# Attention with the product with v a quarter slot later over three buffers, and the shift loaded ahead of the stores

## The reference

```python
q = relu(queries @ Wq_w.T + Wq_b)      # 8 batches x 512 x 128, 16 heads of 8
k = relu(keys @ Wk_w.T + Wk_b)         # one batch, 512 keys
v = relu(values @ Wv_w.T + Wv_b)
score = einsum('bhsd,bhtd->bhst', qh, kh) / sqrt(8)
attn = softmax(score, axis=-1)
a = einsum('bhst,bhtd->bhsd', attn, vh)
```

## Time and profile before

| | |
|---|---|
| median of three runs | 622.29 us (621.78 to 622.56) |
| the profiled execution | 623.81 us, of it a span of 621.3 us in the profile |
| busy over the span | PE 82%, DVE 85%, ACT 64%, POOL 31% |
| products with v (L1492) in the 32 slots | 74.6 to 405.4 us of the span |

### The profile page before, as it was taken

How to read it: one execution, slowest core, us unless ns; L and a number is a source line. 1 busy time by engine, 2 the same in 40 slices (tenths; PEclk the granted TensorE clock), 3 DMA queues, 4 the chain that set the end, 5 groups by cost and what they waited for, 6 DMA issues and landing times.

```text
span 621.3 us, 9777 instructions
## 1 busy us (share of the span) xinstructions
PE 510.5 (82%) x3468; PEld 196.5 (32%) x3475; DVE 526.5 (85%) x879; ACT 395.3 (64%) x773; POOL 194.5 (31%) x309
## 2 busy tenths in 40 slices
PE   1794799999989999999999999877768798888520
PEld 1480122222222222222222222246547664433200
DVE  4769889999999999999999996157998769899976
ACT  1643378898989888888888988525446421144252
POOL 7000212039604544043461318329456330000000
PEclk9997589999999999999999999999988899999965
DMA  9943011111221112121112200010000000000012
GB/s 232 293 141 120 24 27 30 28 38 25 69 61 46 30 32 57 49 59 37 29 36 66 64 23 9 6 50 34 1 2 1 1 1 1 1 0 28 7 34 68
DMA packets 31392, 28.93 MB, mean 47 GB/s; under 512 B 6240, under 2 KB 23784, under 8 KB 31344
## 3 DMA queue, kind: packets, MB, share of 16 engines
q1 hardware_dynamic: 29312, 27.33, 15.1%
q10 hardware_dynamic: 2032, 0.98, 0.6%
HBM read 19.23 MB, written 8.65 MB: 45 GB/s over the span
## 4 chain that ended last, share of the span: by engine, by line
PE 45%; DVE 32%; POOL 7%; ACT 7%; issue 5%; DMA 2%; ACTq 1%; SPq 0%; DVEq 0%
PE ps L1492 14%; PE ps L1487 11%; DVE row_max L1665 10%; PE ps L1460 5%; DVE space L926 4%; PE ps L585 2%; DVE space L862 2%; ACT attended L1613 2%; ACT space L1597 2%; DMA w_in<-in_L_ffn_out_proj_w 1%; DVE st L233 1%; ACT space L830 1%; POOL space L402 1%; POOL space L404 1%; PE ps L342 1%
## 5 line engine op out<-in xcount | busy, mean ns | idle before, releaser
L1665 DVE TENSOR_REDUCE row_max<-ps 128x2 f32<-128x1024 f32 x256 | 299.5, 1220 | 17.0 <-PE ps L1460 14.2
L1597 ACT ACTIVATE space<-ps 128x512 f32<-128x512 f32 x512 | 271.8, 604 | 48.3 <-PE ps L1487 47.9
L1487 PE MATMUL ps<-space 51*128 51x512 bf16 x512 | 159.2, 388 | 7.0 <-ACT space L1597 3.3
L1492 PE MATMUL ps<-space 128*32 128x512 f32 x1024 | 138.1, 612 | 2.9 <-ACT space L1597 0.7
L1460 PE MATMUL ps<-space 48*128 48x512 bf16 x512 | 128.3, 400 | 14.2 <-DVE row_max L1665 12.5
L1487 PEld LDWEIGHTS ps<-space 51*128 51x128 bf16 x512 | 41.1, 94 | 165.1 <-ACT space L1597 144.6
L1333 POOL CAST max_parts<-row_max 128x16 bf16<-128x16 f32 x32 | 6.3, 198 | 236.8 <-DVE row_max L1665 236.8
L585 PE MATMUL ps<-W,space 128*128 128x512 f32 x128 | 66.7, 603 | 0.4
L926 DVE TENSOR_REDUCE space<-ps 128x128 f32<-128x1024 f32 x32 | 38.7, 1221 | 9.1 <-PE ps L585 8.8
L448 POOL TENSOR_TENSOR space<-PC,same_row 128x512 f32<-128x512 f32 x32 | 33.0, 1064 | 35.5 <-DVE PC L876 27.4
L1460 PEld LDWEIGHTS ps<-space 48*128 48x128 bf16 x512 | 26.4, 94 | 56.1 <-DVE row_max L1665 50.2
(11 more groups left out here) (216 smaller groups left out, 623.0 us busy)
## 6 DMA issues: line engine op xcount, KB each, us to landing
q_parts_dram<-space SPq DMA_DIRECT2D x2, 1536.0 KB, 5.4
space<-q_parts_dram SPq DMA_DIRECT2D x64, 48.0 KB
attended_dram<-attended SPq DMA_DIRECT2D x128, 18.0 KB
X<-in_L_attn_queries SPq DMA_DIRECT2D x8, 256.0 KB, 7.7
space<-in_L_ffn_w SPq DMA_DIRECT2D x2, 1024.0 KB, 5.9
space<-q_parts_dram SPq DMA_DIRECT2D x64, 32.0 KB
space<-attended_dram SPq DMA_DIRECT2D x16, 128.0 KB, 2.4
space<-inverses_dram SPq DMA_DIRECT2D x16, 128.0 KB
```

The source lines that it names most:

```text
L1487: pe.matmul(ps[:, col_bank(v), :], k_rows[rows_a, kappa // 4 % 2, tc * P:(tc + 1) * P], q_stack[rows_a, kappa % 4, b * S:(b + 1) * S], sta ...
L1492: mm = pe.matmul(ps[32 * m:32 * m + 32, PV, :], v_heads[:, tc, PAIR * (kappa // 4) + m % PAIR, :], probs[:, tc % 2, m, :], start=(tc == 0) ...
L1597: act.activation(probs[:, tc % 2, m, :], ps[:, col_bank(v), :], ACT.Exp, scale=1.0 / math.sqrt(DH)).then_inc(s_pr, 1)
L1665: dve.tensor_reduce(row_max[:, par].rearrange("p (a c) -> p a c", a=PAIR)[:, :, item], ring(n), AX.X, MAX).then_inc(s_free, 1)
```

## The change

Six things are changed:

1. A third buffer of exponentials in `space8`; quarter `n = 4 kappa + tc` uses buffer `n % 3`.
2. `step` takes at its end the product with v of the quarter before instead of its own; the last product stands behind the loop. Its two waits have moved with it, into `multiply_v`.
3. ScalarE copies bank 7 of slot `kappa - 1` between the exponentials m = 2 and m = 3 of quarter 1 of slot `kappa`, instead of behind the exponentials of quarter 0. The exponential m = 3 and the turned copy now stand behind it.
4. SyncE waits for the turned copy and loads the shift ahead of the wait and the 4 stores of the slot before.
5. The turn of slot 0's maxima is at item 2 of the second eight row scores instead of item 4, with its waits.
6. ScalarE's `copy_attended` for the last slot stands behind the loop.

```diff
-        probs = view(space4, 0, [2, QB, S])
+        probs = [view(space4, 0, [QB, S]), view(space4, QB * S, [QB, S]), view(space8, 0, [QB, S])]
...
+                if kappa + 1 < NQ:
+                    sp.wait_ge(s_pr, turn_item(kappa + 1) + 1)
+                    load_shift(kappa + 1)
+
                 if kappa:
                     sp.wait_ge(s_pve, kappa)
                     store_attended(kappa - 1)
-
-                if kappa + 1 < NQ:
-                    sp.wait_ge(s_pr, turn_item(kappa + 1) + 1)
-                    load_shift(kappa + 1)
...
-            def multiply_v(kappa, tc):
+            def multiply_v(n):
+
+                kappa, tc = n // TC, n % TC
+                if tc == 0 and kappa:
+                    pe.wait_ge(s_pve, kappa)
+                pe.wait_ge(s_pr, column_item(kappa, tc, QB - 1) + 1)
                 for m in range(QB):
                     mm = pe.matmul(ps[32 * m:32 * m + 32, PV, :], v_heads[:, tc, PAIR * (kappa // 4) + m % PAIR, :],
-                                   probs[:, tc % 2, m, :], start=(tc == 0), stop=(tc == TC - 1))
+                                   probs[n % 3][:, m, :], start=(tc == 0), stop=(tc == TC - 1))
                 if tc == TC - 1:
                     mm.then_inc(s_pv, 1)
...
-                if item == 4:
+                if item == 2:
                     pe.wait_ge(s_Wc, 2)
                     pe.wait_ge(s_csum, 1)
                     turn_max(0)
...
-                if tc == 0 and kappa:
-                    pe.wait_ge(s_pve, kappa)
-                pe.wait_ge(s_pr, column_item(kappa, tc, QB - 1) + 1)
-                multiply_v(kappa, tc)
+                if kappa or tc:
+                    multiply_v(TC * kappa + tc - 1)
 
             for kappa in range(NQ):
                 for tc in range(TC):
                     step(kappa, tc)
+            multiply_v(TC * NQ - 1)
...
-            copy_turned(0)
-            exps(0, 0)
-            for kappa in range(NQ):
-                for tc in range(1, TC):
-                    exps(kappa, tc)
-                    if tc == 1 and kappa + 1 < NQ:
-                        copy_turned(kappa + 1)
-                if kappa + 1 < NQ:
-                    exps(kappa + 1, 0)
+            def copy_attended(kappa):
                 act.wait_ge(s_pv, kappa + 1)
-
                 if kappa >= 2:
                     act.wait_ge(s_ast[kappa % 2], 64 * (kappa // 2))
                 act.copy(attended[:, kappa % 2, :], ps[:, PV, :]).then_inc(s_pve, 1)
+
+            copy_turned(0)
+            for kappa in range(NQ):
+                exps(kappa, 0)
+                exps(kappa, 1, range(QB - 1))
+                if kappa:
+                    copy_attended(kappa - 1)
+                exps(kappa, 1, range(QB - 1, QB))
+                if kappa + 1 < NQ:
+                    copy_turned(kappa + 1)
+                exps(kappa, 2)
+                exps(kappa, 3)
+            copy_attended(NQ - 1)
```

More of the change, by code:

```diff
@@ L1591, in copy_turned, with exps @@
                 act.copy(max_turned[:, kappa % 2, :], src).then_inc(s_pr, 1)
-            def exps(kappa, tc):
-                for m in range(QB):
+            def exps(kappa, tc, which=range(QB)):
+                for m in which:
                     v = column_item(kappa, tc, m)
                     act.wait_ge(s_sc, v + 1)
-                    act.activation(probs[:, tc % 2, m, :], ps[:, col_bank(v), :], ACT.Exp,
+                    act.activation(probs[(TC * kappa + tc) % 3][:, m, :], ps[:, col_bank(v), :], ACT.Exp,
                                    scale=1.0 / math.sqrt(DH)).then_inc(s_pr, 1)
-            copy_turned(0)
-            exps(0, 0)
-            for kappa in range(NQ):
-                for tc in range(1, TC):
-                    exps(kappa, tc)
-                    if tc == 1 and kappa + 1 < NQ:
-                        copy_turned(kappa + 1)
-                if kappa + 1 < NQ:
-                    exps(kappa + 1, 0)
+            def copy_attended(kappa):
                 act.wait_ge(s_pv, kappa + 1)
```

## The result

The changed kernel takes 630.26 us (median of 4 runs, 627.68 to 630.86) against 622.07 us before (4 runs, 621.78 to 622.56): a ratio of 1.0117, 95% interval 1.0086 to 1.0147. It is slower, as forecast, but by 8.2 us and not by 1.8, and lies outside the range of 620.0 to 627.0. Two later measurements of the same kernel gave 1.0100 (1.0069 to 1.0131) and 1.0079 (1.0051 to 1.0107).

The account below looks back on a forecast made before the run. The loop of TensorE and ScalarE was taken to set the 2.39 us quarter. Quarters 0 and 1 -0.1, shift +3.1, start -1.35 and end +0.2 gave +1.8 on 622.29: 624.1 us, range 620.0 to 627.0.

Parts of the forecast that it names:

- The wait that the product loses: Normal quarter: column score m = 2 ahead of the product waits for the same count, so it stays 2.39 us; gain 0.
- Quarter 0: Its product no longer waits for the copy of bank 7: 2.55 to 2.39, -0.16 in 22 slots, -3.5 us.
- Quarter 1: The copy waits for the product's end, making exponential m = 3 late: +0.17 in 20 slots, +3.4 us.
- The start: Up to the clock's rise at 81.78 the first product goes away: -1.35 us, bounds -1.9 and 0 (up to +1.4).
- The reload is held up: SyncE's reload waits for the stores' landing, so the shift in slots 9, 17, 25 comes later: +3.1 us.
- PE already waits there, so each counts in full: Slots 9, 17, 25: the shift's delays of 1.09, 1.09 and 0.90 add one to one, +3.1 us.
- signs of being wrong: Prediction wrong if the shift waits have gone, quarter 1 stays at 2.61, or the normal quarter isn't 2.39.
- A: Rival, SyncE's swap: the three waits for the shift go, 618.2 us; chance 0.13.
- B: Rival, quarter 1: the copy fits into ScalarE's gap, starting under 0.96 behind the product, 620.7 us; chance 0.10.
- C: Rival, the start: it gives nothing or costs, 625.5 to 626.9 us; chance 0.12.
- D: Rival, quarter 1: both copies add up, +0.35 instead of +0.17, 627.7 us; chance 0.09.
- E: Rival, stores beside the shift: landing takes over 1.7, 0.5 more in each of three slots, 625.6 us; chance 0.12.

Follow-up runs that it names:

- the moved product: Changed kernel, stores first in slots 8, 16 and 24, with the product moved ahead of column score m = 2: 658.63 us, ratio 1.0572.
- the swap alone: Kernel before with only the shift loaded ahead of the stores: 630.81 us against 623.52, ratio 1.0100.
- the swap in three slots alone: Kernel before with the shift ahead of the stores in slots 8, 16 and 24 only: 636.01 us, ratio 1.0195.
- part 5 undone: Changed kernel with slot 0's turn at item 4 again, single run: 14.35 us from first column score to end of slot 1's first quarter.
- the filling: Changed kernel with 12 more matmuls ahead of TensorE's wait for the shift of slots 10, 18 and 26: 627.86 us, again 627.55.
- the repaired kernels: Changed kernel and kernel before, each with stores first in slots 8, 16, 24 and shift first elsewhere: 620.55 us (0.9947) and 620.85 (0.9960).

## Why the prediction was right or wrong

- **The wait that the product loses buys nothing: right.** The normal quarter is 2.39 before and after. The reason given (column score m = 2 waits for the same count) holds. That the product stays in a loop ahead of column score m = 2 too, with three banks, the moved product shows.
- **Quarter 0, -0.16: right.** 2.39 in all undisturbed slots.
- **Quarter 1, +0.17: right in mechanism, 0.03 too small.** 2.81 - 2.61 = 0.20. The copy started 1.13 behind the product, as in the group that the sum used; the exponential behind it 0.48 later, not 0.46. Together an undisturbed slot is 9.98 against 9.94.
- **The start, -1.35: right in mechanism.** The end of slot 1's first quarter is 14.2 to 14.7 us behind the first column score in eight traces with the changed order, and 15.9 to 16.2 in four with the old one. Where the clock rises equally late (10.3 and 10.5 behind the first column score), it is 14.68 against 16.18, 1.5 us. This place lies one quarter behind that of the forecast and so has quarter 0's 0.16 in it; at the forecast's own place the two differ by 1.34 (12.29 against 13.63). That is the 1.35 of the sum. In the profiled execution the clock rose earlier, 9.6 behind the first column score, and it is 1.67, within the bounds.
- **The reload is held up: right.** The queue shows it, and the swap alone and the swap in three slots alone bring the loss. The delay of the shift was sized too small: forecast 1.09, 1.09 and 0.90, measured from shift to shift 1.36 (slot 9), 1.38 and 1.35 (slots 17 and 25). In slot 9 the reload starts 4.26 behind the shift ahead of it (forecast 4.16, since the landing took 2.73 and not 2.56), and the keys' two issues took 1.05 instead of 0.78. In the slots 17 and 25 it starts 4.28 and 4.29 behind, and the issues between it and the keys take 0.15 and 0.34 longer than before. The sum went by 1.5 us from the last store's issue to the reload; it is 1.6 here (from 159.04 + 3/4 of 1.51 = 160.17 to 161.77), and not the 2.0 that the prediction quoted from the page on DMA. That section of the page is headed as the path of DMAs that GpSimd issues; these stores are SyncE's.
- **"PE already waits there, so each counts in full": this is the step that failed.** The delay was priced one to one, and the lower clock that comes with a longer stall was put at nothing. For the wait itself one to one holds: the shift came 1.36, 1.38 and 1.35 later, and TensorE waited 1.29, 1.35 and 1.34 longer, +4.0 in all where the forecast had 3.1. But with the longer waits came the lower clock, for 17.0 us in this execution, and it cost another 6.3. In five traces (three of the changed kernel, part 5 undone, the swap alone) the 15 waits are 1.75 to 2.72 us long, and 3.4 or 6.8 us at 1.2 GHz came with 11 of them. With the filling, which takes only that away, the three slots are 4.4 to 4.7 us worse than before; without it 10.2 in the profiled execution. I had used the clock for the start and not asked what a longer idle time would do to it in the slots. The rows of the kernel before could have raised the question: the clock stayed up through its waits of 0.54 to 1.43 us, and the prediction made them longer than any of these. None of the signs of being wrong that it names came about, so they could not have caught this.
- **The rivals.** A (the waits go) is wrong for the change, but it is just what the repaired kernels do: 620.55 and 620.85, where the forecast for A was 618.2. B is wrong (1.13 again). C is wrong: the start gave what was forecast or more. D is wrong: 0.20, not 0.35. E is right in direction but small: from the first store to the reload it took 0.2 us longer, not 0.5, and 1.6 from the last issue is under its 1.7.
- The sum, with the measured sizes: start and front -2.2, the waits for the shift +4.0 (6.8 against 2.8), the lower clock +6.3 (5.0 behind the stalls' quarters, 1.3 within them), quarters and end +0.6, behind the slots -0.8: within rounding the 7.8 us of span.

The Trainium skill (TensorE: Matmul & The Clock Gate, Part 1: The HAM clock gate) says that the array's clock follows how busy the engine has lately been. The traces agree: the granted clock fell at or behind most of the longer stalls (waits of 1.75 to 2.72 us), stayed up through stalls as long when they were filled with matmuls, and in the kernel before through the shorter ones.

## What to carry to other kernels

A queue that works in program order hands every wait on to all that is behind it: before two steps are swapped, look for the next instruction in that queue which waits for the *landing* of the one that is moved back, in every slot and not in the typical one. Where that lands in a stall of TensorE, price the stall at more than its length, since the clock may fall behind it; an experiment that fills the stall with harmless matmuls tells the two apart. And where results pass through a ring of n buffers, and the loop through the ring sets the pace, ask where work on the producer will stand between an item and its nth successor before it is moved: here, with three banks, it was in the loop at both places that were run, and the new one was 0.22 us a quarter worse.

## What the runs showed of the hardware

- The lower clock came in stretches of 3.4 us or 6.8 us, and not every time: in the kernel with the swap alone two waits of nearly the same length (1.84 and 1.85 us) ended one without and one with it. The three traces of the changed kernel had it for 17.0, 3.4 and 10.2 us, which cost about 6, 1 and 4 us by the table above.
- With 12 matmuls of 512 columns in the gap the clock stayed at its upper level (granted clock 1.00) in all six stalls of the two traces, and the kernel was not slower for them (627.6 and 627.9 us against 629.4 to 630.3).
- Four stores of 18 KB to DRAM, issued over 1.5 us, let the read behind them start 2.73 us after the first issue here, 2.56 in the last group of the kernel before.
